# A tile's block of counts, turned by one DMA or by two: a graph layer on one Trainium2 core

## The reference, cut to what matters

```python
agg = jax.ops.segment_sum(x[edge_dst], edge_src, num_segments=N_NODES)   # x is layer-normed, 3125 x 256
y = agg + w * x
h = jax.nn.relu(jnp.einsum('nd,hd->nh', y, W1))                          # 256 -> 64
...
```

## Time and profile before

| | us |
|---|---|
| median of 3 runs | 530.05 (529.33 to 532.99) |
| the profiled execution, as timed | 532.43 |
| span of the profiled execution | 530.6 |
| first transposing DMA issued, from the span's start | 86.38 |
| last transposing DMA issued | 207.38 |
| y begins | 217.00 |

### The profile page before, as it was taken

The page is one execution under the profiler, slowest core; times in us unless marked ns, Lnnn a source line. Parts: engine busy times, 40 slices in busy tenths (PEclk is TensorE's granted clock), DMA queues, the critical chain, the costliest instruction groups (busy, mean ns, idle before and its releaser), DMA issues.

```text
span 530.6 us, 12803 instructions
## 1 busy us (share of the span) xinstructions
PE 394.8 (74%) x4336; PEld 355.9 (67%) x4337; DVE 308.6 (58%) x712; ACT 216.2 (41%) x336; POOL 157.7 (30%) x247
## 2 busy tenths in 40 slices
PE   1307765687888886889842499999999999999500
PEld 1306644677887876676742399999999999999400
DVE  5739859757778760455469544444444444444664
ACT  2204315456666664265610254444444354444000
POOL 2158513000000000000000446666666656663300
PEclk9957555889999999988755599999999999999855
DMA  7622006779989899599110112222222222121989
GB/s 178 154 81 50 0 5 112 123 139 173 182 164 173 164 179 180 161 367 338 51 48 0 51 50 80 65 75 69 69 69 69 69 69 79 62 76 51 268 192 294
DMA packets 112754, 63.43 MB, mean 120 GB/s; under 512 B 86333, under 2 KB 106601, under 8 KB 112602
## 3 DMA queue, kind: packets, MB, share of 16 engines
q1 hardware_dynamic: 102388, 43.93, 37.2%
q0 software_dynamic: 7072, 16.00, 9.7%
q10 hardware_dynamic: 3270, 3.20, 1.7%
HBM read 28.76 MB, written 13.85 MB: 80 GB/s over the span
## 4 chain that ended last, share of the span: by engine, by line
PE 53%; DMA 20%; DVE 10%; issue 5%; SPq 5%; ACT 3%; POOL 1%; ACTq 0%; DVEq 0%; POOLq 0%
PE psum L871 18%; PE psum L882 17%; DMA at<-cts 14%; PE psum L743 4%; PE psum L790 3%; PE psum L812 3%; PE psum L734 2%; SPq L281 2%; PE psum L860 2%; DMA w_sb<-pair_rows 2%; PE psum L689 2%; DMA edge_key<-key_f 1%; DMA pair_rows<-yb,scol 1%; PE psum L800 1%; DVE rounds_f L1016 1%
## 5 line engine op out<-in xcount | busy, mean ns | idle before, releaser
L871 PE MATMUL psum<-xgT,w_now 128*128 128x128 f32 x832 | 103.6, 279 | 0.0
L561 ACT CAST cts<-psum 128x1000 bf16<-128x1000 f32 x100 | 78.4, 814 | 57.1 <-PE psum L734 57.0
L871 PEld LDWEIGHTS psum<-xgT,w_now 128*128 128x128 f32 x832 | 99.3, 195 | 0.2 <-issue 0.2
L882 PE MATMUL psum<-w_sb,hT 128*128 x416 | 98.4, 380 | 0.0
L743 PE MATMUL psum<-z,at 125*128 (+1 forms) x1875 | 74.8, 197 | 23.9 <-DMA at<-cts 23.9
L743 PEld LDWEIGHTS psum<-z,at 125*128 125x128 bf16 x1875 | 67.8, 100 | 28.9 <-issue 19.8
L882 PEld LDWEIGHTS psum<-w_sb,hT 128*128 128x128 f32 x416 | 75.1, 190 | 8.4 <-issue 0.3
L647 ACT ACTIVATE hT<-up 128x512 f32<-128x512 f32 x52 | 32.7, 630 | 100.0 <-DVE up L1295 100.0
L470 POOL COPY gcol<-gidx 128x1 int32 (+1 forms) x52 | 9.6, 187 | 210.2 <-DVEq L1260 210.2
L636 ACT COPY w_now<-w_sb 128x1024 f32 x52 | 54.4, 1045 | 32.8 <-DVEq L1260 21.9
L488 POOL DMA_INDIRECT pair_rows<-yb,scol x52 | 51.6, 992 | 47.5 <-issue 34.2
(11 more groups left out here) (219 smaller groups left out, 390.9 us busy)
## 6 DMA issues: line engine op xcount, KB each, us to landing
w_sb<-in_L_ffn_W_dram SPq DMA_DIRECT2D x2, 4096.0 KB, 20.7
res<-in_x_dram SPq DMA_DIRECT2D x5, 560.0 KB
token_rows<-tok SPq DMA_DIRECT2D x5, 560.0 KB
tok<-pair_rows SPq DMA_DIRECT2D x5, 560.0 KB
w_sb<-pair_rows SPq DMA_DIRECT2D x5, 560.0 KB
out_dram<-res ACTq DMA_DIRECT2D x5, 560.0 KB
b_sb<-in_L_ffn_b_dram SPq DMA_DIRECT2D x1, 1024.0 KB, 24.2
xg<-token_rows,gcol POOLq DMA_INDIRECT x52, 2.8
```

The costliest lines, as they stand in the source:

```text
L561: act.copy(cts[:, par, :, d0:d0 + nw * WD].rearrange("p h (b d) -> p b h d", b=nb), psum[:, bank:bank + nb, 0:wb * WC].rearrange("p b (d h ...
L871: last = pe.matmul(psum[:, j % 2, c * P:(c + 1) * P], w1_now[:, j % 2, k, c * P:(c + 1) * P], xgT[:, j % 2, k, :], start=(k == 0), stop=(k ...
L882: last = pe.matmul(psum[:, 4 + j % 2, 0:D], hT[:, j % 2, k, :], w2_sb[:, ds(e, 1), k, :].rearrange("p a h -> p (a h)"), start=(k == 0), st ...
```

## The change

The turned counts of a tile come by two DMAs in place of one, with blocks 0 to 11 and 12 to 24. Each buffer has two semaphores, one per DMA. PE waits for the first ahead of apply share 0, and for the second ahead of apply share 2. ACT, where it waited for one semaphore, waits for both.

```diff
-        at_in, applied, cts_pad = [sem(f"at_in{i}") for i in range(NBUF)], sem("applied"), sem("cts_pad")
+        at_in, applied, cts_pad = [[sem(f"at_in{i}_{k}") for k in range(2)] for i in range(NBUF)], sem("applied"), sem("cts_pad")
...
-        def at_count(r, i, par):
-
-            return at_in[par], (r * FILLED[par] + i + 1) * 16
+        def at_count(r, i, par, half=1):
+
+            return at_in[par][half], (r * FILLED[par] + i + 1) * 16
+
+        PARTS = ((0, 12), (12, NT))
...
-                    sp.dma_start_transpose(at[:, par, :, :],
-                                           cts[:, par, :, :].rearrange("p h d -> p (h d)")).then_inc(at_in[par], 16)
+                    for half, (h0, h1) in enumerate(PARTS):
+                        sp.dma_start_transpose(at[:, par, h0:h1, :], cts[:, par, h0:h1, :].rearrange(
+                            "p h d -> p (h d)")).then_inc(at_in[par][half], 16)
...
                 def tile(kt, i, par):
-                    act.wait_ge(*at_count(r, i - 1, par))
+                    for half in range(2):
+                        act.wait_ge(*at_count(r, i - 1, par, half))
...
                 for par in range(NBUF):
-                    act.wait_ge(*at_count(r, FILLED[par] - 1, par))
+                    for half in range(2):
+                        act.wait_ge(*at_count(r, FILLED[par] - 1, par, half))
...
                 def apply(kt, i, par, c):
-                    if c == 0:
-                        pe.wait_ge(*at_count(r, i, par))
+                    if c % 2 == 0:
+                        pe.wait_ge(*at_count(r, i, par, c // 2))
```

## The result

| | before | after |
|---|---|---|
| median | 531.52 us (529.33 to 536.23, 4 runs) | 514.86 us (510.5 to 515.51, 4 runs) |
| ratio to before | | 0.966, 95% interval 0.957 to 0.975 |
| span of the profiled execution | 530.6 | 513.0 |

A forecast was written before the change was run, and what follows sets the result against it. A latency loop of two tiles, 4.79 us per tile, was taken to bound the kernel. Start 5.6, steady tiles 6.4 and end 1.65 sum to 13.6 us less, giving 516.4 us, range 513 to 524.

The forecast's parts named there:

- What bounds the kernel before: Counts stage: a latency loop of 9.58 us for two tiles, 4.79 per tile, rather than saturated DMA engines.
- The loop goes under, SP's queue is next: Steady tiles: the loop falls to 3.8 us per tile, and SP's queue becomes the bound at 4.31 + s.
- PE still waiting for the first part: Sign of a right prediction: in the stage, SP's wait for ACT's copy is gone while PE still waits for landed counts.
- How large is s: SP's queue: what a second transposing DMA costs besides its blocks; taken as 0.1 us, range 0 to 0.45.
- the slower rival: SP's queue overloaded: s beyond 0.78 us eats the whole gain; with s = 1.08 the time is 536; chance 0.08.
- SP's tile, 4.41: SP's time per steady tile: 4.31 us plus s of 0.1, taken as the changed kernel's bound.
- Start: From the first transposing issue to the sixth tile's: 5.6 us gained, after keeping 1.0 as a loss.
- End: From the last tile's issue to y: 7.95 us in place of 9.62, a gain of 1.65.
- What follows y: All work behind y: shifts with y, its length unchanged.
- Parts landing together: Transfers: the first part's completion is held back behind the second's data; 1.4 us slower, 531.5; chance 0.06.
- A start cost that adds 0.45 to SP's time: SP's queue: start cost near a plain DMA's, SP's tile 4.76 us, 6.6 gained in all, 523.5; chance 0.16.
- A bound between PE, ACT and DVE near 4.6: Steady tiles: PE's shares wait for ACT's copies two shares back, SP's gain is halved, 520; chance 0.08.

The follow-up runs named there:

- two-parts-of-z kernel: Changed kernel, but from the fourth tile on apply uses two of z's three bf16 parts, 50 matmuls in place of 75; 513.3 us, ratio to before 0.967.

## Why the prediction was right, and where it was not

**What bounds the kernel before** was right, by its own steps: a loop of two tiles with 5.67 us of flight and 3.91 from landing to issue, not saturated DMA engines. The kernel with both waits at share 0 keeps the loop and, within 1%, the time.

**The loop goes under, SP's queue is next**: right, by a hair. SP's waits for ACT's copies fell from 12.7 us to 0.2, and the two-parts-of-z kernel shows SP's side as the bound. But PE stands 0.05 us below it and not 0.7 (3.71 against 4.41), and the sign "PE still waiting for the first part" did not come: PE works without a pause.

**How large is s** is the step that failed, in sign and in reasoning. The prediction argued that an issue has no set-up, since data flow from 1.17 us after its begin to 1.18 us after its end, and called the flow "the issue shifted by a constant delay". But the 1.17 us at the begin are SP's own start: a DMA of one block keeps SP for 1.14 us, and no data move meanwhile. The equal 1.18 us at the end have another cause, the blocks by which SP has run ahead. The two could not be told apart with issues of one length only. And the bound from above, 0.45 from plain DMAs, left a start of 1.1 to the slower rival. Such a start is real, dearer than in the rival, and yet hidden: the rival added it to an issue of 3.79 that was itself mostly a wait for the flow. The term SP's tile, 4.41, was mis-sized for the same reason; measured, it is 1.46 + 0.05 + 1.89 + 0.54, or 3.94. Over 19 tiles that makes 9.0 us, the whole of the steady stretch's surplus.

The Trainium skill ("DMA: Bandwidth & Descriptors", "Why a DMA increments its semaphore by 16 and not by 1") gives 631 sequencer cycles for one short transposing DMA from HBM, from which the prediction made an estimate of 0.47 us. Within SBUF, one to six blocks kept SP for 1.14 to 1.21 us here, more than twice that. The fixed cost per block that the prediction worked out of the same table isn't seen in DMAs as short as these: from 1 to 13 blocks the issue grows by 0.34 us in all, from 13 to 24 by 2.16.

**Start**: the number came out, -5.15 for -5.6, but in good part by luck. The kernel with both waits at share 0, which uses nothing early, takes 26.99 us from its first issue at 85.69 to its sixth tile's at 112.68, already 3.8 less than the 30.82 before. Its first tile landed whole at 91.84, the one before only at 94.90, 8.52 after its issue:

```profile
85.69 1.95 SPq L376
...
87.70 4.14 DMA at<-cts
```
```profile
112.68 1.83 SPq L376 DMA_TRANSPOSE at<-cts  x1
```

So no more than some 1.3 of the 5.15 is shown to be the early use's; the rest is mostly a first transfer that was disturbed more in the trace of the kernel before.

**End**: wrong. The last tile's first issue took 2.74 us, and the second part landed 4.24 after its own:

```profile
186.21 2.74 SPq L376
...
189.00 4.24 DMA at<-cts
...
193.29 2.06 PE psum L748 x39
```

A disturbed transfer was in the way, as at the same place before, where the last issue took 4.35: from 186.0 to 187.5 us only 37 GB/s moved. In both traces a packet of the instruction queue falls into it, at 208.4 before and at 185.6 after; whether it is the cause wasn't tested. The forecast's 7.95 us assumed the second part landed 5.80 after the last tile's first issue; it landed after 7.03, which is 1.2 of the 1.6 us missed. The rest is in the 39 matmuls, 2.06 us in place of 1.6, most of them at the 1.2 GHz granted from 193.6.

**What follows y** was taken to shift unchanged; it grew by 4.5 us, with a lower clock. The prediction had looked at the clock only inside the stage.

**The rivals.** Parts landing together: refuted, the first part of a tile lands 3.8 to 4.1 us after its issue in the steady stretch and is used early (the kernel with both waits shows what it would have cost: all). A start cost that adds 0.45 to SP's time: refuted, the pair's 3.42 is below the 3.79. A bound between PE, ACT and DVE near 4.6: PE's bound exists, at 3.88. The range 513 to 524 held the time because 9.0 us more in the steady tiles and 6 less at and behind the end met; that the time lies within 2 us of the forecast is luck, and the reasons would have deserved a wider range.

## What to carry to other kernels

Split a long DMA where its consumer works in order, and let the consumer wait for each piece where it needs it; the split without the later wait gave nothing. Cut into few pieces, each long enough to hide the next one's start: here 12 blocks, which flow for 1.8 us, hid a start of 1.1, and 6 blocks, which flow for 0.9, did not. A first piece of 6 cost 15 us over the 12-block one, and four pieces of 6 or 7 cost 40; nothing between 6 and 12 was tried. And the duration of a DMA issue in a trace is not its cost: a long one may be mostly a wait for the transfer itself, so before it is added up per piece, a row of a short one is needed.

## What the runs showed of the hardware that was not expected

- A transposing DMA's start costs SP about 1.1 us (1.14 for one block of 128x128, 1.21 for six), three times a small plain DMA's 0.38, and no data move in that time (0 GB/s for 1.09 us).
- Behind the start SP issues up to 13 blocks nearly for free (1.48 us in all). Longer issues, 3.64 for 24 blocks and 3.76 for 25, fit a pace set by the flow, 0.15 us a block.
- In the small layers the mean granted clock was 0.82 of full before and 0.76 after, with 4.5 us more; kernels that keep PE's pauses in the stage had 0.83, 0.76 and 0.75 there. With 60 more matmuls, whose results nobody reads, 2.4 GHz was granted from 193.6 to 207.2 us in place of 1.2, and 1.2 GHz from 212.1 on instead, without a gain in the total.
